# Relative-position attention on one core: eight PSUM banks shared out as 3 + 2 + 1 + 2 instead of 2 + 2 + 1 + 3

## The chip, the cores and the metric

The kernel runs on one core of a Trainium2 chip. The metric is the device time in microseconds. Lower is better. TensorE (PE in the profile) multiplies, VectorE (DVE), ScalarE (ACT) and GpSimd (POOL) do the rest, and SyncE (SP) issues the transfers. TensorE writes only to PSUM, which this program holds as eight banks of 128 x 512 fp32.

## The reference: what is computed

A layer on x of shape (8, 1024, 256), fp32, with 16 heads of width 16. The attention has relative-position terms for keys and for values, with distances clipped at 64 in both directions:

```python
q, k, v = proj(Wq, bq), proj(Wk, bk), proj(Wv, bv)        # of layernorm(x)
rk, rv = embK[idx], embV[idx]                              # idx = clip(j - i, -64, 64) + 64
logits = einsum('bhqd,bhkd->bhqk', q, k) + einsum('bhqd,qkd->bhqk', q, rk)
w = softmax(logits)
out = einsum('bhqk,bhkd->bhqd', w, v) + einsum('bhqk,qkd->bhqd', w, rv)
x = x + layernorm(out @ Wo.T + bo)
x = x + layernorm(x @ ternary(W).T + bias)                 # its input is layernorm(x) too
```

## The kernel before

**Steps.** The work is cut into 128 steps: 8 batches, 2 groups of 8 heads, 8 tiles of 128 queries (shifted by 64). Each step handles one tile of queries of 8 heads against all 1024 keys. Four steps form a group of four (`quad`), about 80 us long, 32 in all.

**What a step does.** First, several steps ahead, a row maximum is found. `row_max` (L919 on TensorE) multiplies a cut-down q and k, two heads side by side in the array, into two scores banks: four pairs of heads times two halves of the keys make 8 units, so 16 banks' worth. VectorE reduces each bank to a maximum: halves with the relative band by one fused instruction on scores plus `bands` (L1222, followed by a read of its accumulator), the other halves by a plain maximum (L1216). `row_maxed` counts the emptied banks. `max_rows` (L929) turns the negated maxima, and they are written into the q operand. Then `weights` (L946, with L950 adding the band) computes transposed logits in 16 blocks of 128 x 512, per half of the heads ("blk" 0 and 1) four of kind X and four of kind Y. The first two X blocks are "near": each of their four bf16 matmuls has an fp32 transpose of a band behind it. The others are "far", of four matmuls. ScalarE takes the exponential of each block (L1424) into `wl` and `wm` for near blocks, and `wr` and `wy` for far ones. `weighted` (L970) multiplies by the values into the bank `oacc`, X after the four X blocks, Y after the four Y blocks. `merge` (L1245) folds `wl` into `wm`.

**Small products.** Everything else TensorE does goes through the banks called `misc`, one user at a time: `band_raw` (L902, read by ScalarE in two copies, L1403 and L1404), `max_rows` (L929, read at L1235 and L1237), at the end of a group of four `relative` (L982, two parts of four pieces each, read by L1254 into `relout`) and `relative_sum` (L995, read by L1263), `out_norm` (L1006, read up to L1279), per finished tile of rows the tail products (L1020 read by L1437, L1034 read by L1292 or L1333), and per chunk of 256 tokens of the next batch the projections (L865, L875, L883, L892).

**Banks.** `NLOG, NMISC, NSCORE` give the counts for logits, small products and scores; `oacc` is the eighth bank. In `row_max` TensorE waits, for side 0 and 1 of the unit that starts with bank number u:

```python
pe.wait_ge(row_maxed, u + side - NSCORE + 1)
mm = e.matmul(scores[(u + side) % NSCORE][:, c % 512:c % 512 + length], ...
```

**What sets the order.** Each engine runs one fixed list of instructions, in order. `timetable` gives every stage of every step a place on a common scale (one unit is one head of one step; 32 units for a group of four) from the table `PLACES`; `order_of` sorts each engine's list by place plus the engine's lag from `LAG` (`END_LAG` for the last four tiles). `with_banks` goes through the stages in that order, gives each small product the bank that is free first, takes it as occupied for `HOLD` units, and pushes a product to a later place where no bank is free by this plan. `misc_banks` then finds for each the count of the reader that it must wait for. `HOLD` is a planning number only: the waits in the program are on the real readers. SyncE's queue is one such list too, for every load, store and band transfer.

Of the kernel before, what the change touches and what calls it, by code (L numbers as in the profile page):

```python
# [11 lines left out]
ACT = mybir.ActivationFunctionType  # L12
# [33 lines left out]
LOWEST = -3.0e38  # L46
QRING, BRING, VRING, MRING = 5, 7, 3, 3
HB = HG // 2
NLOG, NMISC, NSCORE = 2, 3, 2


def tile_of(s):
# [51 lines left out]
def own_root(stage, k):  # L104
# [1 line left out]
    return k == (0, 0) if stage == "statistics" else last_tile(*k) and k[1] % 2 == 1  # L106


PLACES = {'chunk': (61.05, 71.03, 81.0, 91.0),
 'load_x': -8.23,  # L110
 'statistics': -5.34,
 'normalise': -2.6,
 'turn_x': 0.38,
 'project_q': 1.18,
 'project_v': 10.3,
 'far': 4.0,
 'write_q': 6.3,
 'project_k': 5.53,
 'write_far': 7.8,
# [1 line left out]
 'first_chunk': (-100.0, -90.0, -80.0, -70.0),  # L121
 'first_statistics': (-108.7, -102.4, -102.27, -102.4),
 'first_normalise': (-103.3, -99.5, -89.5, -79.5),
 'first_stages': (-0.27, 0.5, 2.6, 4.4, 4.8, 5.83, 6.2, 6.3),
 'keys_first_stages': (0.0, 4.0, 4.8, 0.0, 3.0, 8.5, 7.3, 5.33),
 'first_load_k': (-84.0, -73.9, -63.8, -62.01),
 'first_load_q': (-89.0, -77.2, -65.4, -53.6),
 'first_raw': -54.47,
 'step': 7.2,
 'half': 3.55,  # L130
 'load_k': (-41.8, -33.8, -25.8, -17.8),
 'first_load_mk': (-83.9, -73.8, -63.8, -63.5),
 'load_mk': (-41.7, -33.7, -25.7, -17.7),
 'load_mq': -21.5,
 'first_load_mq': (-88.17, -77.1, -65.3, -53.5),
 'load_q': -32.7,
 'raw': (-28.8, -25.4),
 'band_write': (-26.3, -22.8),
 'band_read': (-22.18, -20.26),
 'row_max': (-12.49, -11.62, -10.75, -9.88, -9.01, -8.14, -7.1, -6.4),  # L140
 'max_reduce': -6.0,
 'max_rows': -4.88,
 'max_move': -5.05,
 'near': (0.0, 0.4, 0.72, 0.98),
 'rest': (1.76, 2.1, 2.5, 2.9),
 'value_x': 2.3,
 'value_y': 4.1,
 'merge': 3.2,
 'out_copy': 7.6,
 'relative': (29.57, 31.07),  # L150
 'piece_by': 0.35,
 'sum': (33.0, 33.95),
 'norm': (35.6, 36.59),
 'tail': 38.0,
 'tail_by': 8.0,
 'tail_late_by': 6.5,
 'tail_load': -1.0,
 'tail_attT': 0.21,
 'tail_wo': 1.0,
 'tail_x1': 3.0,  # L160
 'tail_norm': 3.5,
 'tail_normed': 5.4,
 'tail_x1T': 10.15,
 'tail_ff': 11.3,
 'tail_out': 13.5,
 'tail_store': 15.82,
 'end': 36.6,
 'end_by': 0.65,
 'end_stages': (0.3, 0.41, 2.27, 2.4, 3.4, 4.3, 4.7, 7.0, 6.8)}


def timetable():

    slots, x_ = [], PLACES

# [92 lines left out]
def with_banks(slots):  # L268
# [12 lines left out]
    while queue:  # L281
        slot, i, planned, stage, k = queue.pop()
        chain, bank = chain_of(stage, k), None
        if slot < planned + late.get(chain, 0):
            put_back((planned + late[chain], i, planned, stage, k))
            continue
        if stage in HOLD:
            if stage == "relative" and k[2]:
# [8 lines left out]
            if stage == "relative":  # L297
                held = bank
            until[bank] = slot + (10 if stage == "relative" and k[2] < 3 else HOLD[stage])
        timed.append((slot, stage, k, bank))  # L300
# [5 lines left out]
 'DVE': {'project_v': 0.17,  # L306
         'out_norm': 0.7,
         'tail_wo': 0.7,
         'tail_x1': 1.06,
         'tail_norm': 1.4,  # L310
         'tail_normed': 3.2,
         'tail_out': 1.9},
 'ACT': {'turn_x': -0.23, 'far': 0.4, 'project_q': 1.2, 'band_raw': -0.04},
 'POOL': {'project_q': 3.4,
          'project_k': 2.0,
          'far': 2.0,
# [6 lines left out]

END_LAG = {'PE': {},
 'SP': {},
 'DVE': {'tail_wo': 0.28, 'tail_ff': 0.5},
 'ACT': {'tail_attT': 0.2, 'tail_x1T': 1.0},
 'POOL': {'tail_wo': 0.95, 'tail_norm': 0.35, 'tail_ff': 0.86}}

# [1 line left out]
def order_of(engine, slots):  # L331


    def lag(stage, k):
# [22 lines left out]
            "project_v": "v_ready", "band_raw": "praw_ready", "max_rows": "nm_ready", "relative": "rel_ready",  # L357
            "relative_sum": "o_added", "out_norm": "attn_ready", "tail_attT": "rows_ready", "tail_x1T": "rows_ready",
            "tail_wo": "lin_ready", "tail_ff": "lin_ready", "ternary": "threshold_ready"}
HOLD = {'turn_x': 0.8,  # L360
 'project_q': 2.0,
 'project_k': 2.0,
 'far': 1.4,
 'project_v': 1.8,
 'band_raw': 0.8,
 'max_rows': 0.9,
 'relative': 1.0,
 'relative_sum': 1.4,
 'out_norm': 1.83,
 'tail_attT': 0.6,  # L370
 'tail_x1T': 0.5,
 'tail_wo': 1.3,
 'tail_ff': 1.3,
 'ternary': 2.0}


def counts(orders):
# [1186 lines left out]
```

## Time and profile before

| | us |
|---|---|
| median of 3 runs | 2714.83 |
| lowest, highest | 2706.01, 2718.36 |
| the profiled execution, whole | 2715.1 |
| its span, first to last instruction | 2713.3 |
| TensorE matmul row busy | 2488.4 (92%) |
| TensorE weight loads busy | 1778.2 (66%) |
| VectorE busy | 2098.3 (77%) |
| ScalarE busy | 1563.9 (58%) |
| GpSimd busy | 949.4 (35%) |

The first 100 us or so fill the pipeline, with projections of the first batch and many transfers; the last 60 us finish the last rows. Between them the pattern of a group of four repeats. A matmul stands in the trace twice, as a weight load (PEld) and as a matmul (PE), whose end is modelled; in brackets stands the idle time of the row in front of it and who ended it.

### The profile page before, as it was taken

The numbers are of one execution on the slowest core, as the hardware profiler recorded it, in microseconds if no ns is written. First come the engines' busy times: TensorE is split into PE (matmuls) and PEld (weight loads), VectorE is DVE, ScalarE is ACT, GpSimd is POOL, SyncE is SP. The second block draws the span as 40 slices with busy tenths as digits, with TensorE's granted clock in tenths as the row PEclk, the third lists the DMA queues.
The fourth block names the chain that finished last, engine by engine and source line by source line (L and its number), as shares of the span: only waits on it lengthen the run. The fifth ranks groups of instructions, "written<-read, shape, count | busy, mean of one in ns | idle before, by whom it ended". The sixth has DMA issues, their size and how long they took to land. (4 is left out here: it accounts for less than half of the span.)

```text
span 2713.3 us, 101117 instructions
## 1 busy us (share of the span) xinstructions
PE 2488.4 (92%) x41858; PEld 1778.2 (66%) x41858; DVE 2098.3 (77%) x5306; ACT 1563.9 (58%) x2993; POOL 949.4 (35%) x2211
## 2 busy tenths in 40 slices
PE   5599999999999999999999999999999999999995
PEld 3266766667666676667666676666766667666664
DVE  5577778877888778877788777887778877787776
ACT  2266665566666555666556665556665655566652
POOL 3001533335342443424334253343524244341014
PEclk8699999999999999999999999999999999999997
DMA  6765674657656575566655666456764657656510
GB/s 162 210 162 160 184 185 132 163 161 204 167 148 168 156 196 155 148 164 178 183 140 157 172 187 177 138 145 167 209 168 132 164 168 192 164 141 178 142 42 29
DMA packets 696147, 434.22 MB, mean 160 GB/s; under 512 B 215847, under 2 KB 695431, under 8 KB 695559
## 3 DMA queue, kind: packets, MB, share of 16 engines
q1 hardware_dynamic: 695686, 427.75, 57.3%
q8 instruction: 330, 5.41, 0.9%
q14 instruction: 131, 1.07, 0.1%
HBM read 231.91 MB, written 194.92 MB: 157 GB/s over the span
## 5 line engine op out<-in xcount | busy, mean ns | idle before, releaser
L946 PE MATMUL logitsT<-qs,ks 98*128 98x128 bf16 (+1 forms) x8192 | 952.9, 222 | 31.5 <-ACT wr L1424 11.6
L1222 DVE CUSTOM_DVE_ANT_1 junk<-scores,bands 128x512 bf16<-128x512 f32 x988 | 680.3, 689 | 270.4 <-PE scores L919 115.4
L1424 ACT ACTIVATE wy<-logitsT 128x512 f32<-128x512 f32 x1024 | 589.5, 597 | 419.8 <-PE logitsT L946 408.7
L1216 DVE TENSOR_REDUCE maxes<-scores 128x1 f32<-128x512 f32 x1024 | 657.3, 683 | 173.3 <-PE scores L919 171.0
L946 PEld LDWEIGHTS logitsT<-qs,ks 98*128 98x128 bf16 (+1 forms) x8192 | 576.0, 99 | 306.6 <-issue 172.2
L919 PE MATMUL scores<-mks,mqs 48*128 48x256 bf16 (+6 forms) x3712 | 518.8, 291 | 121.1 <-DVE maxes L1216 62.5
L950 PE MATMUL logitsT<-ident,bands 128*128 128x128 f32 x2048 | 407.9, 280 | 0.0
L1424 ACT ACTIVATE wr<-logitsT 128x512 f32<-128x512 f32 x512 | 293.5, 596 | 163.6 <-PE logitsT L946 157.4
L919 PEld LDWEIGHTS scores<-mks,mqs 48*128 48x128 bf16 (+1 forms) x3712 | 162.9, 94 | 333.7 <-DVE maxes L1216 111.2
L1453 POOL TENSOR_SCALAR rs<-rs 128x1 int32<-128x1 int32 (+1 forms) x217 | 42.2, 195 | 898.9 <-DVE rs L1097 888.4
L950 PEld LDWEIGHTS logitsT<-ident,bands 128*128 128x128 f32 x2048 | 295.8, 144 | 24.9
L1458 POOL TENSOR_SCALAR rs<-rs 128x1 f32<-128x1 f32 x744 | 282.4, 382 | 64.9
L970 PE MATMUL oacc<-wy,vs 128*17 128x128 f32 (+1 forms) x9216 | 277.1, 264 | 0.7 <-ACT wy L1424 0.7
L1463 POOL TENSOR_SCALAR rs<-rs 128x1 f32<-128x1 f32 x744 | 217.5, 295 | 66.1
L970 PEld LDWEIGHTS oacc<-wy,vs 128*17 128x17 f32 x9216 | 207.1, 98 | 37.5 <-issue 9.4
L1424 ACT ACTIVATE wl<-logitsT 128x512 f32<-128x512 f32 x256 | 158.4, 619 | 117.7 <-PE logitsT L950 116.4
L1424 ACT ACTIVATE wm<-logitsT 128x512 f32<-128x512 f32 x256 | 154.3, 603 | 83.0 <-PE logitsT L950 78.4
L1403 ACT ACTIVATE praw<-misc 128x512 f32<-128x512 f32 x256 | 153.4, 599 | 64.7 <-DMA bs<-praw 44.0
L1245 DVE COPY_PREDICATED wm<-later,wl 128x512 f32<-128x512 int32 x224 | 175.7, 784 | 2.2 <-PE oacc L970 2.2
L970 PE MATMUL oacc<-wr,vs 128*17 128x128 f32 (+1 forms) x4608 | 161.6, 264 | 0.0
L1404 ACT ACTIVATE praw<-misc 128x512 f32<-128x512 f32 x256 | 156.3, 611 | 0.0
L970 PEld LDWEIGHTS oacc<-wr,vs 128*17 128x17 f32 x4608 | 118.1, 100 | 0.1
(147 smaller groups left out, 2977.5 us busy)
## 6 DMA issues: line engine op xcount, KB each, us to landing
bs<-praw SPq DMA_DIRECT2D x256, 512.0 KB, 4.3
bands<-bs SPq DMA_DIRECT2D x224, 512.0 KB, 4.4
ks<-kd SPq DMA_DIRECT2D x64, 384.0 KB, 4.8
qs<-qd SPq DMA_DIRECT2D x112, 192.0 KB
bands<-bs SPq DMA_DIRECT2D x128, 128.0 KB, 3.3
mks<-kd SPq DMA_DIRECT2D x128, 96.0 KB, 3.9
qd<-qparts SPq DMA_DIRECT2D x60, 192.0 KB, 2.6
kd<-kparts SPq DMA_DIRECT2D x60, 192.0 KB, 2.6
```

Of the source, the lines that this page charges most:

```text
L919: mm = e.matmul(scores[(u + side) % NSCORE][:, c % 512:c % 512 + length], mqs[i][HALF * side:HALF * side + depth, p, :], kk[HALF * side:HA ...
L946: mm = e.matmul(lt[:, j * P:(j + 1) * P], kk[0:depth, SLOT[HB * blk + j], kt * P:(kt + 1) * P], qs[i][0:depth, SLOT[HB * blk + j], :], sta ...
L950: mm = e.matmul(lt[:, j * P:(j + 1) * P], band[v % BRING][:, j, c * P:(c + 1) * P], ident[:], start=False, stop=True, is_transpose=True, s ...
L970: mm = e.matmul(oacc[32 * j:32 * j + VW, o0 + q0:o0 + q1], vs[m_ % VRING][:, int(right), kt, h, :], src, start=first and c == 0, stop=True ...
L1216: e.tensor_reduce(top, sc[:], AX.X, ALU.max).then_inc(row_maxed, 1)
L1222: e.tensor_tensor_reduce(junk[:], sc[:].rearrange("p (a c) -> p a c", a=2), banded, 1.0, LOWEST, ALU.add, ALU.max, top).then_inc(row_maxed, 1)
L1245: e.copy_predicated(right, mask.bitcast(I32), left).then_inc(merged, 1)
L1403: e.activation(dst[:, :, 0:P], src, ACT.Copy)
L1404: e.activation(dst[:, :, P:WIN], src[:, :, P - 1:P].broadcast_to([P, HB, P]), ACT.Copy).then_inc(praw_ready, 1)
L1424: e.activation(dst, src, ACT.Exp).then_inc(exp_ready, 1)
L1458: op = e.tensor_scalar(rs[k][:, 3, x:x + 1], rs[k][:, 2, x:x + 1], rs[k][:, 0, x:x + 1], rs[k][:, 2, x:x + 1], ALU.mult, ALU.mult)
L1463: op = e.tensor_scalar(rs[k][:, 2, x:x + 1], rs[k][:, 3, x:x + 1], 1.5, rs[k][:, 2, x:x + 1], ALU.add, ALU.mult)
```

## The change

The counts become `NLOG, NMISC, NSCORE = 2, 2, 3`: three scores banks used in turn, and two small banks. No instruction's arithmetic changes and no instruction is added or removed. With NSCORE 3 a unit's side 0 waits until all banks up to three before its own are emptied, where it was two.

The numbers of `PLACES`, `LAG`, `END_LAG` and `HOLD` are set anew. Most move by a few hundredths to tenths of a unit. Those that change orders visibly:

```diff
-NLOG, NMISC, NSCORE = 2, 3, 2
+NLOG, NMISC, NSCORE = 2, 2, 3
@@ PLACES
- 'near': (0.0, 0.4, 0.72, 0.98),
- 'rest': (1.76, 2.1, 2.5, 2.9),
+ 'near': (0.0, 0.76, 0.72, 0.98),
+ 'rest': (1.76, 2.1, 2.5, 2.77),
- 'first_load_mq': (-88.17, -77.1, -65.3, -53.5),
+ 'first_load_mq': (-83.18, -73.73, -61.06, -50.13),
- 'sum': (33.0, 33.95),
+ 'sum': (33.44, 34.25),
@@ HOLD
- 'band_raw': 0.8,
- 'max_rows': 0.9,
- 'relative': 1.0,
- 'relative_sum': 1.4,
+ 'band_raw': 0.2,
+ 'max_rows': 0.23,
+ 'relative': 0.25,
+ 'relative_sum': -0.12,
```

All entries of `HOLD` shrink in this way, so the plan lets a product follow its bank's last user sooner.

TensorE at the end of a group of four, where the two parts of `relative` (`misc<-wm,reltab`) stand between scores, a row turn (`misc<-ident,attn`) and the output projection (`misc<-wo,rowsT`). The number behind a name is the bank or buffer. Before:

```order
L1020 MATMUL misc1<-ident,attn0 128x128
L1020 MATMUL misc1<-ident,attn1 128x128
L982 MATMUL misc0<-wm,reltab 32x64 x16
L1034 MATMUL misc2<-wo,rowsT 128x256 x2
L919 MATMUL scores0<-mks0,mqs2 128x512
L919 MATMUL scores1<-mks0,mqs2 128x512
L982 MATMUL misc1<-wm,reltab 32x64 x24
```

And after:

```order
L982 MATMUL misc0<-wm,reltab 32x64 x16
L1034 MATMUL misc1<-wo,rowsT 128x256 x2
L919 MATMUL scores0<-mks0,mqs2 128x512
L919 MATMUL scores1<-mks0,mqs2 128x512
L982 MATMUL misc0<-wm,reltab 32x64 x24
```

The 16 end part 0 and the 24 are the first three pieces of part 1. Part 1 had bank 1, while part 0 was still being read in bank 0; now both use bank 0 one after the other. The row turn has moved up ahead of these rows.

TensorE a little later, inside a step, from the end of the second near block to the last X block. Before:

```order
L946 MATMUL logitsT1<-qs2,ks0 128x128
L950 MATMUL logitsT1<-ident,bands 128x128
L946 MATMUL logitsT0<-qs2,ks0 128x128 x4
L919 MATMUL scores0<-mks0,mqs2 128x512
L919 MATMUL scores1<-mks0,mqs2 128x512
L946 MATMUL logitsT1<-qs2,ks0 128x128 x4
```

After, with the first far block in front of the near one (whose four pairs are left out here but for the first):

```order
L1020 MATMUL misc1<-ident,zbuf0 128x128 x2
L982 MATMUL misc0<-wm,reltab 32x64 x8
L946 MATMUL logitsT1<-qs2,ks0 128x128 x4
L946 MATMUL logitsT0<-qs2,ks0 128x128
L950 MATMUL logitsT0<-ident,bands 128x128
```

The far block has moved ahead of the near block; behind the near block follow the scores unit and the last far block, as before.

VectorE at the same end of a group, at the reader of part 0 (`relout<-misc0`) between two reductions. Before:

```order
L1222 ISA maxes1 128x1
L1326 TENSOR_SCALAR zbuf0<-x1_0,mv2,rs2 128x256
L1254 TENSOR_TENSOR relout<-misc0,relmask 128x8x32x2
L1216 TENSOR_REDUCE maxes1<-scores0 128x1
L1216 TENSOR_REDUCE maxes1<-scores1 128x1
L1292 TENSOR_TENSOR ybuf<-misc2,bo 128x256
```

After:

```order
L1222 ISA maxes1 128x1
L1254 TENSOR_TENSOR relout<-misc0,relmask 128x8x32x2
L1326 TENSOR_SCALAR zbuf0<-x1_0,mv2,rs2 128x256
L1216 TENSOR_REDUCE maxes1<-scores0 128x1
L1216 TENSOR_REDUCE maxes1<-scores1 128x1
L1292 TENSOR_TENSOR ybuf<-misc1,bo 128x256
```

The reader has moved up by one operation.

## Rows read from the trace of the kernel before

**Rows 1.** The page, part 1: busy us, share of the span, instructions.

```profile
PE 2488.4 (92%) x41858; PEld 1778.2 (66%) x41858; DVE 2098.3 (77%) x5306; ACT 1563.9 (58%) x2993; POOL 949.4 (35%) x2211
```

**Rows 2.** Waits of the matmul row: us in total, times, longest us.

```profile
PE scores L919 <- DVE maxes L1216: 62.5, 200, 1.6
PE scores L919 <- DVE maxes L1222: 28.4, 65, 2.9
```

**Rows 3.** Waits of the weight loads, whole span.

```profile
PEld scores L919 <- DVE maxes L1216: 111.2, 274, 1.8
PEld logitsT L946 <- ACT wr L1424: 72.9, 237, 0.7
PEld scores L919 <- DVE maxes L1222: 72.2, 169, 3.2
...
PEld logitsT L946 <- ACT wy L1424: 20.3, 80, 0.6
...
PEld logitsT L946 <- ACT wm L1424: 13.3, 49, 0.9
```

**Rows 4.** Timeline: start us, us, engine, line, count, [idle before].

```profile
1101.23 0.70 PE L919 MATMUL scores<-mks,mqs 48*128 48x256 bf16 x4
...
1101.54 0.11 PEld L919 LDWEIGHTS scores<-mks,mqs 48*128 48x128 bf16 x3 [0.22 <-DVE maxes L1216]
```

**Rows 5.** Waits of the weight loads in the first 150 us.

```profile
PEld scores L919 <- DVE maxes L1222: 13.1, 13, 3.2
PEld scores L919 <- DVE maxes L1216: 9.4, 16, 1.8
```

**Rows 6.** Groups by line: out<-in, count | busy, mean ns | idle before.

```profile
L1222 DVE CUSTOM_DVE_ANT_1 junk<-scores,bands 128x512 bf16<-128x512 f32 x988 | 680.3, 689 | 270.4 <-PE scores L919 115.4 <-issue 58.3 <-DMA bands<-bs 26.2
L1216 DVE TENSOR_REDUCE maxes<-scores 128x1 f32<-128x512 f32 x1024 | 657.3, 683 | 173.3 <-PE scores L919 171.0
...
L1222 DVE DVE_READ_ACCUMULATOR2_ANT maxes<- 128x1 f32 x1024 | 84.6, 83 | 0.0
```

**Rows 7.** Waits of the weight loads in one group of four, 1071.4 to 1149.9.

```profile
PEld scores L919 <- DVE maxes L1216: 3.7, 9, 0.7
PEld scores L919 <- DVE maxes L1222: 2.4, 8, 0.6
```

**Rows 8.** Timeline of the weight loads of scores at that group's end.

```profile
1142.17 0.09 PEld L919 LDWEIGHTS scores<-mks,mqs 48*128 48x128 bf16 x1 [0.67 <-DVE maxes L1216]
1142.77 0.22 PEld L919 LDWEIGHTS scores<-mks,mqs 48*128 48x128 bf16 x5 [0.51 <-DVE maxes L1216]
1144.09 0.09 PEld L919 LDWEIGHTS scores<-mks,mqs 48*128 48x128 bf16 x1 [0.21 <-DVE maxes L1222]
1144.83 0.09 PEld L919 LDWEIGHTS scores<-mks,mqs 48*128 48x128 bf16 x1 [0.65 <-DVE maxes L1222]
```

**Rows 9.** Busy time by stretch: from:to, length, engines, clock, DMA share, GB/s.

```profile
1071.40:1149.90 78.50, 74.97 (x1240) 53.49 (x1238) 68.32 (x181) 47.27 (x90) 33.05 (x92) 1.00 0.49 137
1141.00:1149.00 8.00, 6.83 (x140) 4.41 (x141) 7.51 (x19) 3.06 (x6) 4.27 (x12) 1.00 0.23 76
```

**Rows 10.** Timeline: the reader of part 0 on VectorE, part 1 on TensorE.

```profile
1148.20 0.68 DVE L1254 TENSOR_TENSOR relout<-misc,relmask 128x512 f32<-128x512 f32 x1
1148.83 1.08 PE L982 MATMUL misc<-wm,reltab 128*32 128x64 f32 x48
```

**Rows 11.** Timeline: two exponentials in a row, and the logits behind them.

```profile
1113.16 1.25 ACT L1424 ACTIVATE wr<-logitsT 128x512 f32<-128x512 f32 x2 [0.66 <-PE logitsT L946]
1114.47 0.23 PEld L946 LDWEIGHTS logitsT<-qs,ks 101*128 101x128 bf16 x4 [0.41 <-ACT wr L1424]
```

**Rows 12.** Groups by line: the second of the two readers of `band_raw`.

```profile
L1404 ACT ACTIVATE praw<-misc 128x512 f32<-128x512 f32 x256 | 156.3, 611 | 0.0
```

**Rows 13.** Timeline of TensorE at the start.

```profile
82.67 0.61 PE L919 MATMUL scores<-mks,mqs 51*128 51x512 bf16 x2 [17.11 <-DMA mks<-kd]
```

More of the change, by code:

```diff
@@ L106, in own_root @@
     return k == (0, 0) if stage == "statistics" else last_tile(*k) and k[1] % 2 == 1
-PLACES = {'chunk': (61.05, 71.03, 81.0, 91.0),
+PLACES = {'chunk': (61.72, 71.69, 81.66, 91.62),
  'load_x': -8.23,
@@ L112 @@
  'normalise': -2.6,
- 'turn_x': 0.38,
+ 'turn_x': 0.25,
  'project_q': 1.18,
- 'project_v': 10.3,
- 'far': 4.0,
+ 'project_v': 10.09,
+ 'far': 4.52,
  'write_q': 6.3,
@@ L123 @@
  'first_normalise': (-103.3, -99.5, -89.5, -79.5),
[L124 to L127, printed above, removed]
+ 'first_stages': (-0.3, 0.47, 2.57, 4.15, 4.77, 5.8, 6.17, 6.83),
+ 'keys_first_stages': (0.0, 4.0, 4.8, 0.08, 3.0, 8.5, 7.3, 5.33),
+ 'first_load_k': (-83.61, -73.9, -63.8, -62.01),
+ 'first_load_q': (-89.0, -77.2, -64.9, -53.6),
  'first_raw': -54.47,
@@ L130 @@
  'half': 3.55,
- 'load_k': (-41.8, -33.8, -25.8, -17.8),
- 'first_load_mk': (-83.9, -73.8, -63.8, -63.5),
- 'load_mk': (-41.7, -33.7, -25.7, -17.7),
+ 'load_k': (-41.8, -33.8, -25.8, -17.84),
+ 'first_load_mk': (-83.13, -73.03, -63.03, -62.73),
+ 'load_mk': (-41.8, -33.7, -25.7, -17.91),
  'load_mq': -21.5,
- 'first_load_mq': (-88.17, -77.1, -65.3, -53.5),
+ 'first_load_mq': (-83.18, -73.73, -61.06, -50.13),
  'load_q': -32.7,
  'raw': (-28.8, -25.4),
- 'band_write': (-26.3, -22.8),
+ 'band_write': (-26.51, -22.8),
  'band_read': (-22.18, -20.26),
@@ L143 @@
  'max_move': -5.05,
- 'near': (0.0, 0.4, 0.72, 0.98),
- 'rest': (1.76, 2.1, 2.5, 2.9),
+ 'near': (0.0, 0.76, 0.72, 0.98),
+ 'rest': (1.76, 2.1, 2.5, 2.77),
  'value_x': 2.3,
- 'value_y': 4.1,
+ 'value_y': 4.12,
  'merge': 3.2,
- 'out_copy': 7.6,
+ 'out_copy': 7.74,
  'relative': (29.57, 31.07),
- 'piece_by': 0.35,
- 'sum': (33.0, 33.95),
- 'norm': (35.6, 36.59),
+ 'piece_by': 0.37,
+ 'sum': (33.44, 34.25),
+ 'norm': (35.47, 36.59),
  'tail': 38.0,
@@ L157 @@
  'tail_load': -1.0,
- 'tail_attT': 0.21,
+ 'tail_attT': -0.28,
  'tail_wo': 1.0,
@@ L161 @@
  'tail_norm': 3.5,
- 'tail_normed': 5.4,
+ 'tail_normed': 5.5,
  'tail_x1T': 10.15,
@@ L167 @@
  'end': 36.6,
- 'end_by': 0.65,
- 'end_stages': (0.3, 0.41, 2.27, 2.4, 3.4, 4.3, 4.7, 7.0, 6.8)}
+ 'end_by': 0.66,
+ 'end_stages': (0.3, 0.41, 2.11, 2.32, 3.4, 4.16, 4.7, 7.0, 6.85)}
 def timetable():
@@ L308 @@
          'tail_wo': 0.7,
-         'tail_x1': 1.06,
+         'tail_x1': 0.88,
          'tail_norm': 1.4,
@@ L312 @@
          'tail_out': 1.9},
- 'ACT': {'turn_x': -0.23, 'far': 0.4, 'project_q': 1.2, 'band_raw': -0.04},
+ 'ACT': {'turn_x': -0.23, 'far': 0.4, 'project_q': 1.2, 'band_raw': -0.13},
  'POOL': {'project_q': 3.4,
@@ L325 @@
  'SP': {},
- 'DVE': {'tail_wo': 0.28, 'tail_ff': 0.5},
+ 'DVE': {'tail_wo': 0.28, 'tail_ff': 0.5, 'tail_norm': 0.22, 'tail_x1': -0.12},
  'ACT': {'tail_attT': 0.2, 'tail_x1T': 1.0},
@@ L359 @@
             "tail_wo": "lin_ready", "tail_ff": "lin_ready", "ternary": "threshold_ready"}
[L360 to L364, printed above, removed]
- 'band_raw': 0.8,
- 'max_rows': 0.9,
- 'relative': 1.0,
- 'relative_sum': 1.4,
[L369 to L374, printed above, removed]
+HOLD = {'turn_x': 0.06,
+ 'project_q': 1.25,
+ 'project_k': 0.92,
+ 'far': 0.45,
+ 'project_v': 0.45,
+ 'band_raw': 0.2,
+ 'max_rows': 0.23,
+ 'relative': 0.25,
+ 'relative_sum': -0.12,
+ 'out_norm': 0.75,
+ 'tail_attT': 0.15,
+ 'tail_x1T': 0.12,
+ 'tail_wo': 0.75,
+ 'tail_ff': -0.34,
+ 'ternary': 0.5}
 def counts(orders):
```

## The prediction

> **What bounds the kernel now.** I read the page first [rows 1]: TensorE's matmul row is busy for 2488.4 of 2713.3 us, VectorE's for 2098.3. TensorE's own queue sets the time; VectorE is the next. Then I asked who TensorE waits for. Its matmul row waits for `maxes` (VectorE's row maximum, which frees a scores bank) for 62.5 + 28.4 = 90.9 us [rows 2]. That understates it, because matmul ends are modelled. The weight loads in front of the same matmuls wait 111.2 + 72.2 = 183.4 us for `maxes` in 274 + 169 waits, and those of `logitsT` wait 72.9 + 20.3 + 13.3 = 106.5 us for the exponentials [rows 3]. An instance: before 1101.54 the load waits 0.22 us for `maxes` while the matmul row reads as busy, 0.70 us for four matmuls [rows 4]. I take the load row as the real stall. Of the 183.4 us, 13.1 + 9.4 = 22.5 us lie in the first 150 us [rows 5], where other things set the pace; 161 us lie in the steady part. The rows of the small products name inputs that they wait for, hardly ever the reader of an earlier product, so three small banks are enough now.
>
> **Part 1, a third scores bank.** A unit of `row_max` fills two banks (two heads), and VectorE empties each in 0.683 us, or in 0.689 + 0.083 = 0.77 us with the bands [rows 6]. With two banks TensorE can be one unit ahead only when both are emptied; with three it gets one bank, so 0.68 to 0.77 us, more lead. How much of a wait this removes depends on whether waits stand alone or in trains, for within a train the lead is spent once. I counted in one group of four steps, 1071.4 to 1149.9: 17 waits, 3.7 + 2.4 = 6.1 us [rows 7]. Three places are larger than one bank: the train 0.67 + 0.51 + 0.21 + 0.65 = 2.04 us at 1142 to 1145 [rows 8], and two units with two waits each of the same kind, 0.80 us at 1105 and 0.74 at 1123. Taking 0.68 off each leaves 0.12 + 0.06 + 1.36 = 1.5 us; the others stand apart, are at most 0.50 us and go. So 4.6 of 6.1, three quarters, is removed: 0.75 x 161 = **-121 us**. From below it is three quarters of the matmul row's waits, 0.75 x 90.9 = -68, less a tenth for the head, -61; from above all 161.
>
> **Part 2, carry-over.** VectorE is busy 68.32 of 78.50 us in that group, and 7.51 of the 8.00 us from 1141 to 1149, across the train [rows 9]. Once TensorE comes earlier, VectorE's backlog is larger at the next unit, and part of the removed wait returns. Nothing shows how much: nothing at least, 50 us at most (then VectorE's idle time shrinks from 10.2 us a group by only 2.2). I take a fifth of part 1, **+25 us**.
>
> **Part 3, near and far blocks.** `near` moves the second near block (four pairs of bf16 and fp32 matmuls) from in front of the first far block to behind it, so the two far X blocks no longer stand together. Today they do: two exponentials take 1.25 us in a row, and the next block of logits waits 0.41 us for the bank at 1114.47 [rows 11]. In the new order the far block's exponential, 0.60 us, runs beside the near block. It also puts the second values product (`wy`) of the step before one near block sooner behind its exponentials; no wait of that kind stands in the rows now, and some may come. I take **-15 us** of the 106.5; bounds are -50 (about half of it) and +30, since TensorE, held up less by VectorE, reaches these two banks earlier and ScalarE's 0.6 us per block is unchanged.
>
> **Part 4, two small banks instead of three.** 990 small products pass through them. A bank comes free when the reader is done: for `band_raw` two copies of 0.6 us on ScalarE, for `relative` one of 0.68 us [rows 10, 12], with VectorE's queue in front: 1 to 2 us in all. I counted in the order, spacing TensorE's rows as the trace does, how much other work stands between a bank's use and its next use. Under 1.0 us: 11 products before, 28 after. Under 1.5 us: 19 and 118. Under 2.0 us: 50 and 219. The median falls from 6.0 to 3.6 us. The new places thus use the work between well but leave a hundred products at the limit. The case to look at is `relative`: part 1 now goes into the bank of part 0, and must wait for its reader. In the trace part 1 starts at 1148.83 and that reader ends at 1148.20 + 0.68 = 1148.88 [rows 10], so this costs little, and the reader moves ahead of one VectorE operation. About 118 x 0.3 us = **+35 us**. Bounds: 28 x 0.5 = +14; 219 x 0.5 = +110, if readers are late as behind VectorE's backlog at 1142.
>
> **Part 5, the rest.** `HOLD`, the lags and most places only decide the orders counted above. At the start, SP issues the q writes of a chunk ahead of loads of `mqs`, and `mks` behind the k writes. TensorE waits there until 82.67, 17.11 us, for `mks` [rows 13]; that comes from the last chunks, and the issues ahead of these are the same in number. 0, within 5 us either way. The last 60 us pass through two small banks instead of three; the tail of the last rows waits for normalisations, not for banks. 0, within 5 us.
>
> **Sum.** 2713.3 - 121 + 25 - 15 + 35 = 2637 us of span. The execution took 2715.1, so 1.8 us lie outside: 2639, rounded to **2640 us**. It is as good against the median, 2714.8, from which the profiled run differs by 0.3 us. A measurement of this kernel can tell about 0.5%, 13.6 us, from no change.
>
> **Rivals.**
> A, the full gain (10%). All waits for `maxes` go, part 3 gives its -30, and small banks cost their least: 2715 - 161 - 30 + 14 + 10 = 2548 us. For it: most waits are shorter than one bank's 0.68 us. Against it: the train at 1142. The Trainium skill (Perfetto Trace Analysis, Matmuls) says that independent matmul groups should rotate through different banks so that emptying one overlaps the next group; by that rule alone this would be the case to expect.
> B, VectorE is the bound (13%). The gain is the lower end of part 1, -61, then +25 for the carry-over and +35 for the banks: 2715 - 61 + 60 = 2714 us, no change. For it: 87% of VectorE busy in the group shown. Against it: elsewhere it is less, and 10.2 us of idle time are left in this group.
> C, slower (12%): the small banks stop TensorE's queue. A small product that waits holds up all logits and scores behind it, VectorE and ScalarE run dry, the backlog then delays the next reader. At 219 products x 0.8 us = 175 us, less 121, with 25 carried over, it gives 2715 + 79 = 2794 us. It decides from 96 us of new waits on, 0.44 us for each of the 219. Against it: the places leave a median of 3.6 us. The Trainium skill (Perfetto Trace Analysis, Optimization Strategy) reads the same gap, repeated on the engine that should be full, as a sign of too few PSUM buffers; the trace shows it today at the scores and not at the small products, and the rule warns of both.
>
> **How the numbers follow.** The forecast, 65%, has 2590 to 2690 as its own range. A is 10%, B 13%, C 12%. The range 2575 to 2712 holds the forecast's case with its tails, half of B and a part of A; C and the far end of A are left out. Faster by over 0.5% (under 2701): 0.65 + 0.10 + 0.01 = 0.76. Within 0.5%: 0.12. Slower: 0.12.
>
> **What would show it.** In the profile after: loads of `scores` waiting for `maxes` about 50 to 80 us instead of 183.4 (part 1 with its carry-over), what is left standing at the end of each group of four steps; `logitsT` loads waiting 70 to 110 us for ScalarE; new rows of small products waiting for `praw`, `nm`, `relout`, `vs` or `attn`, together about 35 us and none over 15. VectorE's busy share should rise from 77% to 79 or 80. I am wrong in part 1 if the `maxes` waits stay above 110 us, and in part 4 if small products wait over 70 us.

## The result, and the profile after

The kernel after takes **2569.24 us** (median of 4, 2568.3 to 2575.28), the kernel before 2710.73 in the same comparison (median of 4, 2706.01 to 2718.36). The ratio is **0.948**, with 0.945 to 0.951 as its 95% interval: 141.5 us less. The forecast was 2640, its low end 2575. So the sign was right, and the time is 6 us below the range. One of the ten executions behind experiment x1 below ran at a mean clock of 0.646 and took 3245.83 us; it is left out of every number here.

The page after, part 1 (rows 1 are the same line of before):

```profile
PE 2413.4 (94%) x41858; PEld 1747.5 (68%) x41858; DVE 2072.1 (81%) x5306; ACT 1564.0 (61%) x2993; POOL 955.9 (37%) x2211
```

The instruction counts are the same. The span is 2568.1 us, 145.2 less. TensorE's busy time fell by only 75.0 us (its row can read as busy while a load waits, as [rows 4] showed), and its idle time by 70.2. VectorE's share is 81%, where I had forecast 79 or 80.

The waits of the weight loads after (us in total, times, longest us), to be held against [rows 3]:

```profile
PEld logitsT L946 <- ACT wr L1424: 59.0, 243, 0.4
...
PEld scores L919 <- DVE maxes L1222: 30.2, 67, 1.3
PEld scores L919 <- DVE maxes L1216: 29.2, 80, 1.0
...
PEld logitsT L946 <- ACT wm L1424: 23.7, 103, 0.4
...
PEld misc L982 <- DVE relout L1254: 9.9, 14, 1.0
...
PEld misc L995 <- DVE relout L1254: 6.6, 10, 3.4
```

The waits for `maxes` fell from 111.2 + 72.2 = 183.4 us to 29.2 + 30.2 = 59.4. This -124 is the largest change of any wait. Of it, 13 lie in the first 150 us (22.5 to 9.5, [rows 5]) and 111 behind them (160.9 to 49.9). `logitsT` waits for ScalarE went from 106.7 us (the 106.5 of [rows 3] and 0.2 for `wl`) to 59.0 + 23.7 + 11.3 (`wy`) + 1.7 (`wl`) = 95.7. Against both stands a wait that before did not have: `relative` (L982) waits for `relout`, 9.9 us in 14 waits. The matmul row understates here as it did in [rows 2]; after, it shows

```profile
PE scores L919 <- DVE maxes L1216: 12.6, 39, 0.8
PE scores L919 <- DVE maxes L1222: 10.8, 22, 1.0
```

**Where along the span.** The first group of four starts at 113 us in both kernels, and the end takes 110 and 109 us. All of the gain is therefore in the groups of four. They come in four kinds, by what else they carry; the shortest of each kind took 78.4, 75.9, 85.3 and 79.5 us before and 74.9, 70.5, 83.2 and 76.0 after. Two neighbours in the windows view (from:to, length, busy time and count of PE, PEld, DVE, ACT, POOL, clock, DMA share, GB/s):

```profile
1022.60:1097.50 74.90, 73.13 (x1239) 52.47 (x1236) 67.47 (x181) 47.55 (x90) 33.10 (x92) 1.00 0.54 153
1097.50:1168.30 70.80, 68.33 (x1340) 49.39 (x1332) 58.98 (x151) 46.09 (x85) 17.45 (x46) 1.00 0.69 190
```

Before, the first of them is the first of [rows 9], and the second this:

```profile
1149.90:1228.20 78.30, 73.67 (x1335) 52.10 (x1334) 59.45 (x151) 46.92 (x87) 18.42 (x47) 0.96 0.62 170
```

In the first group VectorE's busy time is nearly the same (68.32 and 67.47 us) and the group is 3.6 us shorter, so VectorE now fills 90% of it (67.47 of 74.90), where it was 87%. In the second the gain is 7.5 us; note the clock, 0.96 before and 1.00 after.

The train of [rows 8] at the end of the first group has become this (timeline of the weight loads):

```profile
1090.26 0.22 PEld L919 LDWEIGHTS scores<-mks,mqs 48*128 48x128 bf16 x5 [0.60 <-DVE maxes L1216]
...
1092.09 0.09 PEld L919 LDWEIGHTS scores<-mks,mqs 48*128 48x128 bf16 x1 [0.42 <-DVE maxes L1222]
...
1096.51 0.89 PEld L982 LDWEIGHTS misc<-wm,reltab 128*32 128x32 f32 x48 [0.69 <-DVE relout L1254]
```

2.04 us of waits for `maxes` are now 0.60 + 0.42 = 1.02, so 1.02 went, more than one bank's 0.68. The sum over the group is 1.8 + 0.8 = 2.6 instead of 6.1 [rows 7]; beside the train six single waits of 0.19 to 0.49 us are left. The last row is a price of having only two small banks: part 1 stands still for 0.69 us until part 0 is read out.

### The profile page after: what moved, and what is told of

It is laid out like the page before. It is cut to its first block, busy times and chain, and to the rows that moved or that the text cites. A ratio compares the mean times of both kernels' runs of the same rounds, so it can differ in the third digit from the quotient of the medians.

```text
span 2568.1 us, 101028 instructions
## 1 busy us (share of the span) xinstructions
PE 2413.4 (94%) x41858; PEld 1747.5 (68%) x41858; DVE 2072.1 (81%) x5306; ACT 1564.0 (61%) x2993; POOL 955.9 (37%) x2211
## 4 chain that ended last, share of the span: by engine, by line
PE 54%; DVE 13%; issue 4%; ACT 3%; POOL 1%; DMA 0%; SPq 0%; DVEq 0%; ACTq 0%; POOLq 0%
PE logitsT L946 13%; PE oacc L970 12%; PE scores L919 7%; PE logitsT L950 6%; DVE junk L1222 4%; DVE maxes L1216 4%; PE misc L1034 3%; PE misc L875 3%; PE misc L995 2%; PE misc L892 2%; PE misc L902 1%; ACT wr L1424 1%; PE misc L982 1%; DVE stats L1092 1%; PE misc L1006 1%
## 5 line engine op out<-in xcount | busy, mean ns | idle before, releaser
L946 PE MATMUL logitsT<-qs,ks 98*128 98x128 bf16 (+1 forms) x8192 | 915.7, 221 | 21.8 <-ACT wr L1424 8.8
L1424 ACT ACTIVATE wy<-logitsT 128x512 f32<-128x512 f32 x1024 | 581.4, 597 | 332.3 <-PE logitsT L946 321.1
L946 PEld LDWEIGHTS logitsT<-qs,ks 98*128 98x128 bf16 (+1 forms) x8192 | 562.4, 99 | 274.9 <-issue 150.4
L919 PE MATMUL scores<-mks,mqs 48*128 48x256 bf16 (+6 forms) x3712 | 448.5, 289 | 36.8 <-DVE maxes L1216 12.6
L1424 ACT ACTIVATE wr<-logitsT 128x512 f32<-128x512 f32 x512 | 305.3, 596 | 200.2 <-PE logitsT L946 191.6
L1453 POOL TENSOR_SCALAR rs<-rs 128x1 int32<-128x1 int32 (+1 forms) x217 | 48.6, 224 | 803.3 <-DVE rs L1097 793.8
L919 PEld LDWEIGHTS scores<-mks,mqs 48*128 48x128 bf16 (+1 forms) x3712 | 138.9, 94 | 196.9 <-DVE maxes L1222 30.2
L1424 ACT ACTIVATE wm<-logitsT 128x512 f32<-128x512 f32 x256 | 152.9, 597 | 24.6 <-PE logitsT L950 3.8
L902 PE MATMUL misc<-bandtab,qs 96*128 96x128 bf16 x1024 | 100.3, 220 | 20.3 <-ACT praw L1404 14.5
```

Of the source, the lines that this page charges most:

```text
L946: mm = e.matmul(lt[:, j * P:(j + 1) * P], kk[0:depth, SLOT[HB * blk + j], kt * P:(kt + 1) * P], qs[i][0:depth, SLOT[HB * blk + j], :], sta ...
L1424: e.activation(dst, src, ACT.Exp).then_inc(exp_ready, 1)
```

## The experiments

The runs are called x1 to x12. **The theory** (L in the expectations) was the prediction's with a larger first term: the third scores bank is worth well over 100 us, the two small banks cost little, and the new orders alone bring little. **Its rival** (O): the orders brought the gain, and the banks only came along. Two facts of the program make a clean table possible. The new tables give the same order of instructions on every engine whether the counts are 2, 2, 3 or 2, 3, 2 or 2, 2, 2 (only the numbers of the banks differ), and the old tables with the new `HOLD` keep TensorE's order of before but for a few products at the very end. So order and banks can be changed apart.

### New order, two scores banks and two small ones

```diff
 # after
-NLOG, NMISC, NSCORE = 2, 2, 3
+NLOG, NMISC, NSCORE = 2, 2, 2
```

> The changed kernel with NLOG, NMISC, NSCORE = 2, 2, 2: the new orders, two small banks, and the third scores bank taken away again. The instruction order of each engine is the changed kernel's, only the waits differ. Theory L (the lead of the third bank carries the gain, about 105 to 125 us of it, the clock's dips with it): 2680 to 2700 us, weight loads of scores waiting 150 to 190 us for maxes. Theory O (the new orders carry most of the gain, the bank little): 2590 to 2620 us, with waits for maxes under 100 us.

Measured (x1): 2698.79 us (median of nine), ratio to before 0.9959 (0.994 to 0.9979).

```profile
PEld scores L919 <- DVE maxes L1216: 109.1, 274, 1.2
PEld scores L919 <- DVE maxes L1222: 92.3, 224, 1.3
```

201.4 us of waits for `maxes` against 59.4 after: 142 us, and the time differs by 130 us. The waits are above the 150 to 190 us that I expected. In the matmul row the same waits are 62.0 + 36.8 = 98.8 us, against 23.4 after: 75 us, which is too little for the 130.

### New order, banks shared out as before

```diff
 # after
-NLOG, NMISC, NSCORE = 2, 2, 3
+NLOG, NMISC, NSCORE = 2, 3, 2
```

> The changed kernel with the counts of before, 2, 3, 2: the new orders alone. Theory L: 2665 to 2690 us, so 20 to 45 us under the kernel before, from fewer costly neighbours on TensorE and the near and far blocks; it lies 0 to 20 us under the run with 2, 2, 2, which is the price of the small bank. Theory O: 2580 to 2610 us.

Measured (x2): 2691.91 us, ratio 0.9927 (0.9903 to 0.995), just above the range. The orders alone give 20 us. The third small bank is worth 7 us in this order, which is not told apart from none: the intervals of x1 and x2 overlap. The waits for `maxes` are 109.6 + 95.9 = 205.5 us, 22 more than before: what the new order saves elsewhere, TensorE partly gives back at the scores banks.

### Old order, banks shared out as after

```diff
 # before
-NLOG, NMISC, NSCORE = 2, 3, 2
+NLOG, NMISC, NSCORE = 2, 2, 3
 # and HOLD as after
```

> The kernel before with the counts 2, 2, 3 and the new HOLD, which leaves TensorE's order as it was but for the last few products: the banks alone. Theory L: 2590 to 2630 us; the waits for maxes fall from 183 to 60 to 90 us, small products wait 10 to 40 us more. Theory O: 2680 to 2710 us. If the third bank and the new orders only work together, it stays above 2660 although the run of new orders alone does too.

Measured (x3): 2629.03 us, ratio 0.9693 (0.9664 to 0.9722).

```profile
PEld scores L919 <- DVE maxes L1216: 42.3, 96, 1.6
PEld scores L919 <- DVE maxes L1222: 26.7, 79, 1.1
PEld misc L982 <- DVE relout L1254: 24.5, 27, 1.4
```

### Old order, two banks for all

```diff
 # before
-NLOG, NMISC, NSCORE = 2, 3, 2
+NLOG, NMISC, NSCORE = 2, 2, 2
 # and HOLD as after
```

> The kernel before with 2, 2, 2 and the new HOLD: the order of before with one small bank less and nothing for it. The prediction put this price at 35 us (14 to 110): 2725 to 2820 us. If small banks are as cheap as the profile after suggests, 2715 to 2730 us. Beside the run with the old order and 2, 2, 3 it gives the worth of the third scores bank a second time.

Measured (x4): 2738.08 us, ratio 1.0104 (1.0073 to 1.0135). `relative` waits 12.0 us for `relout` here, and small products in all 88 us instead of 47.5. The matmul row's waits for `maxes` are 87.3 us here and 24.6 in x3: again too little, 63 us, for the 109 us between the two runs.

**The table these four complete** (medians in us; in brackets the weight loads' waits for `maxes`):

| logits, small, scores | old order | new order |
|---|---|---|
| 2, 3, 2 | 2712 (183) | 2692 (206) |
| 2, 2, 2 | 2738 (179) | 2699 (201) |
| 2, 2, 3 | 2629 (69) | 2569 (59) |

Down the last step, the third scores bank is worth 109 us in the old order and 130 in the new one, and the waits for `maxes` fall by 110 and 142: nearly one for one. Some of it is clock: the mean granted clock in the middle of the runs is 0.973 in x4 and 0.977 to 0.978 in x3, 0.976 in x1 and 0.979 after, by my estimate 12 and 8 us. The step above it, the third small bank given up, costs 26 and 7 us. Across, the new order brings 20 us with 2, 3, 2, then 39 with 2, 2, 2 and 60 with 2, 2, 3. So the theory stands for the banks: -20 + 7 - 130 = -143. Its part on the orders was too small. They are worth 21 us more with the third scores bank than without it, and 19 us more with two small banks than with three.

### What in the orders: the near and far blocks

```diff
 # after
- 'near': (0.0, 0.76, 0.72, 0.98),
+ 'near': (0.0, 0.4, 0.72, 0.98),
```

> The changed kernel with near set back to (0.0, 0.4, 0.72, 0.98): both near blocks in front of both far X blocks again, the rest as changed. The prediction gave this edit 15 us: 2575 to 2595 us. If the 60 us between the old order and the new order with three scores banks (2629 and 2569) lie mostly in near, 2610 to 2630 us.

Measured (x5): 2579.05 us, ratio 0.9501 (0.9483 to 0.952): 10 us more than after by the medians, 6 by the ratios, whose intervals overlap. `logitsT` waits for ScalarE 98.4 us against 95.7.

```diff
 # before, with the banks and HOLD of after
- 'near': (0.0, 0.4, 0.72, 0.98),
+ 'near': (0.0, 0.76, 0.72, 0.98),
```

> The kernel before with 2, 2, 3, the new HOLD and only near set anew: near alone on the old order. If near is most of the 60 us, 2570 to 2590 us. If it is the 15 us of the prediction, 2605 to 2625 us, and the rest lies in the places of scores and small products.

Measured (x6): 2624.22 us, ratio 0.9657 (0.9628 to 0.9687), against 0.9693 without the edit. The two runs point the same way and each alone is within its uncertainty. A small gain, some 5 to 10 us.

### What in the orders: three groups of places, each put into the kernel of x3

First the projections of the next batch (`chunk` moves their loads, statistics and stores with them):

```diff
 # before, with the banks and HOLD of after
-PLACES = {'chunk': (61.05, 71.03, 81.0, 91.0),
+PLACES = {'chunk': (61.72, 71.69, 81.66, 91.62),
- 'turn_x': 0.38,
+ 'turn_x': 0.25,
- 'project_v': 10.3,
- 'far': 4.0,
+ 'project_v': 10.09,
+ 'far': 4.52,
```

> The old order with 2, 2, 3 (2629 us) and only the places of the projections set anew (chunk, turn_x, project_v, far). Between that kernel and the changed one lie 60 us; the near blocks gave 5 to 10 of them. If the rest lies in the places of small products, this run takes a part: 2605 to 2625 us, with the waits of small products at 80 to 95 us instead of 102.

Measured (x9): 2594.97 us, ratio 0.9559 (0.9531 to 0.9587), 34 us less than 2629.03 and 10 us below the range that I expected.

```profile
PEld misc L982 <- DVE relout L1254: 10.4, 14, 1.1
```

`relative`'s waits for `relout` go from 24.5 us in 27 waits to 10.4 in 14, all waits of small products from 102 to 79 us. Nothing of `relative` itself was moved, only the work of the projections, some of which uses the same two banks. The waits that are gone stood at two of a batch's four groups of four, 9.4 us in the one with most of the projections and 5.4 in the one at whose end they begin; the other two have 9.6 us in x3 and 10.5 in x9. So more than half of that stall hung on where the projections stand. Whether they took `relative`'s bank or delayed its reader in VectorE's queue, this run does not separate.

Then the small products of the step and the tail (`piece_by`, `sum`, `norm`, `out_copy`, `tail_attT`, `tail_normed`, the `end` places, `LAG`, `END_LAG`):

```diff
 # before, with the banks and HOLD of after
- 'sum': (33.0, 33.95),
- 'norm': (35.6, 36.59),
+ 'sum': (33.44, 34.25),
+ 'norm': (35.47, 36.59),
...
- 'tail_attT': 0.21,
+ 'tail_attT': -0.28,
```

> The old order with 2, 2, 3 and the places of the other small products set anew: relative, its sums, out_norm, the tail, and the lags. Expected if the order around relative and its reader is the cost of two small banks: 2590 to 2615 us, loads of relative waiting for relout 8 to 15 us instead of 24.5. If it stays above 2620, the 60 us lie elsewhere.

Measured (x10): 2633.65 us, ratio 0.9708 (0.9683 to 0.9734). No gain: 5 us more than x3, not told apart from none. The waits for `maxes` fell by 15 us (53.9 against 69.0) and the time did not follow. The trace shows two things behind that. It has 30.7 us at half clock in its steady part, where x3 has 10.2. And the four kinds of groups went different ways (the shortest full one of each, taken here from the last load of `relative` to the next): the kind without projections and the one at whose end they begin are shorter than in x3, 75.2 against 75.8 us and 70.7 against 71.3; the kind with most of them and the one in which they end are longer, 87.3 against 86.2 and 77.7 against 76.9.

And the logits' and values' places:

```diff
 # before, with the banks and HOLD of after
- 'near': (0.0, 0.4, 0.72, 0.98),
- 'rest': (1.76, 2.1, 2.5, 2.9),
+ 'near': (0.0, 0.76, 0.72, 0.98),
+ 'rest': (1.76, 2.1, 2.5, 2.77),
- 'value_y': 4.1,
+ 'value_y': 4.12,
```

> The old order with 2, 2, 3 and near, rest and value_y set anew, the whole order of logits. near alone gave 5 us (2624). rest moves one far Y block by 0.13 units, so that two Y blocks stand together before the scores unit: 2605 to 2625 us. If it falls under 2600, the order of logits against scores is the larger part of the 60 us.

Measured (x11): 2622.90 us, ratio 0.9667 (0.9641 to 0.9693), as with `near` alone. Of the 60 us between x3 and after, the projections carry 34, these places some 6, the small ones none by themselves. About 20 us belong to no group alone. By the same measure after is shorter than x9 in all four kinds of groups, by 0.4 to 0.9 us each (70.8 to 70.1, 83.8 to 83.4, 76.9 to 76.1, 75.8 to 74.9); eight groups of each come to some 22 us. That fits small products whose gain of 0.6 us a group in x10 shows once the projections stand elsewhere. It was not tested, and the load places, which none of the three had, may have a part; this stays open.

### The waits for `maxes` themselves, shortened at their source

Both kernels with the plain maximum over a quarter of its bank, which makes VectorE's reader faster and leaves the banks as they are:

```diff
 # before (x7) and after (x8), L1216
-  e.tensor_reduce(top, sc[:], AX.X, ALU.max).then_inc(row_maxed, 1)
+  e.tensor_reduce(top, sc[:, 0:128], AX.X, ALU.max).then_inc(row_maxed, 1)
```

> The kernel before, but the plain maximum (L1216) reads 128 of the 512 columns of its bank, so the row maximum leaves out three quarters of half of the keys; TensorE's work is unchanged. VectorE gets some 450 us less work. Theory L (the weight loads' waits for maxes, 183 us, are what the two banks cost): waits fall under 60 us and the time to 2560 to 2600 us. If the matmul row's 91 us were the true size, it would stay at 2620 or above.

Measured (x7): 2581.23 us, ratio 0.951 (0.9492 to 0.9527).

```profile
PEld scores L919 <- DVE maxes L1222: 49.4, 108, 3.2
...
PEld scores L919 <- DVE maxes L1216: 6.4, 21, 0.8
```

The load row's waits for `maxes` fall by 183.4 - 55.8 = 127.6 us and the time falls by 134. The matmul row had only 90.9 us of such waits to give [rows 2]. The near match is not exact evidence: VectorE also has 393 us less work (2098.3 to 1705.5), and other waits of the load row rise (`logitsT` and `oacc` for ScalarE by 18 us, transfers by 28). But x4 against x3 and x1 against after, where only a bank changes, say the same, 110 and 142 us of waits for 109 and 130 us of time. So the load row has nearly the true size of this stall, and the matmul row half of it.

> The changed kernel with the same short maximum (L1216 reads 128 of 512 columns; three quarters of half of the keys are left out of the row maximum). Waits for maxes are 59 us there now. Theory L: they fall to 10 to 30 us and the time to 2525 to 2550 us, 20 to 45 us under the changed kernel. If VectorE still sets the pace of the changed kernel through other waits, it gains over 60 us.

Measured (x8): 2524.82 us, ratio 0.9295 (0.9269 to 0.9321): 44 us less than after, where 26 us of the waits for `maxes` go (59.4 to 33.4) and 14 of small products' waits (76.7 to 62.6). So a faster VectorE is still worth something after the change, a third of what it was, and by these waits the scores banks are some 26 us of the 44.

### A value product one step of the table sooner

```diff
 # after
- 'value_x': 2.3,
+ 'value_x': 2.0,
```

> The changed kernel with value_x at 2.0 instead of 2.3: the first values product between the first and the second Y block, where TensorE waits for ScalarE today (27 us before the second Y block). If that wait is hidden by it: 2545 to 2565 us. If the product itself now waits for the last X exponential, and the later Y blocks stand closer together: 2570 to 2600 us, with more waits of oacc for ScalarE.

Measured (x12): 2631.57 us, ratio 0.9695 (0.967 to 0.972), 62 us more than after. A miss in size.

```profile
PEld logitsT L946 <- ACT wy L1424: 73.0, 205, 0.6
...
PEld oacc L970 <- ACT wr L1424: 36.6, 132, 0.5
```

The value product now stands ahead of its exponential (`wr`) and waits 132 times; behind it in TensorE's queue stand logits, so ScalarE gets its next block late, and then the logits wait for `wy`, 73.0 us where after has 11.3. Moving one stage by 0.3 units costs almost half of what the third bank brings.

## Why the prediction was right or wrong

**The reading of the bound was right.** TensorE's queue set the time, and its largest stall was the wait for `maxes`, 183.4 us by the load row. The pairs x4 and x3, x1 and after confirm the choice of the load row.

**The sizes of the waits that I had priced came near.** What was missing lies outside them. Each is taken from the sums of the weight loads' waits, before and after:

| | forecast | measured |
|---|---|---|
| parts 1 and 2: `scores` for `maxes`, from 150 us on | -121 + 25 = -96 | 160.9 to 49.9: -111 |
| the same in the first 150 us | left out | 22.5 to 9.5: -13 |
| part 3: `logitsT` for ScalarE | -15 | 106.7 to 95.7: -11 |
| part 4: small products for readers and inputs on VectorE and ScalarE | +35 | 47.5 to 76.7: +29 |
| values (`oacc`) for ScalarE | named in part 3, not priced | 2.7 to 11.4: +9 |
| everything else | 0 | -48 |

The "else" completes the span's 145.2 us: the load row's own busy time is 30.7 us less (1778.2 to 1747.5, the same 41858 loads), waits for transfers are 7 less, waits named "issue" 4 less, and 7 lie in gaps too short to be listed.

**Part 5, everything else at 0, is the first step that failed.** By this table 48 us lie there. Two things had no term of their own.

One is the orders: "most places only decide the orders counted above". I had priced one visible swap, at -15, and added it to the banks as if neither depended on the other. The new order is worth 20 us with the banks of before, 39 with two banks for each use and 60 with the banks of after. 34 of these 60 are the projections', to whose places I gave no term. They stand mostly in one of the four kinds of groups, but in x3 more than half of `relative`'s 24.5 us of waits for its bank went when they alone were moved. A little of what they give is the clock: the trace of x3 has 10.2 us at half clock in its steady part, that of x9 none, so 5 us at most.

The other is the clock. The mean granted clock is 0.971 in the middle of 14 runs of before (0.965 to 0.976) and 0.979 in those of after; 0.008 of some 2640 us is about 20 us, an estimate. I looked for waits alone, and the sum had no term for it. It is not all of the busy time that the load row lost: the profiled executions of x1 and after have the same mean clock, 0.979, and the loads take 1768.0 and 1747.5 us. So some 20 of the 30.7 us came with the third scores bank at an equal clock; why the loads themselves get shorter with fewer waits is not shown.

**Part 2, the carry-over, is the second: a guess, too large.** In the group that I had priced it fits: 3.5 of 6.1 us went, and 4.6 less a fifth is 3.7. The train kept 1.02 us where 1.36 was expected, but six single waits stayed that were to go. Over the whole steady part 69% of the waits went (111 of 160.9), more than the 60% that three quarters less a fifth come to, and so 10 of the 25 us are left for a carry-over. The 13 us of the first 150 us were left out although the third bank works there too. The prediction also contradicted itself: it expected 50 to 80 us of these waits to be left, and 183.4 less the gross 121 is 62, with the charge 87. The Trainium skill (Perfetto Trace Analysis, Matmuls) says to rotate independent matmul groups through different PSUM banks. This case agrees, with 109 to 130 us for a third bank.

**Part 3 came near partly by luck.** `near`, the edit that it priced, gives 3 us of these waits in the new order (98.4 in x5, 95.7 after) and 5 in the old one (114.5 in x3, 109.2 in x6). The third scores bank in the old order adds 9 (105.6 in x4, 114.5 in x3), as the reason for the upper bound had it; the rest of the new order takes that back.

**Part 4, the two small banks, was right in kind, and its size is luck.** The waits are +29 us against +35, and the row named ahead, `relative` for its bank, is the largest of its kind, 9.9 us; no new one is over 15. But from x2 to x1, where only the third small bank goes, they rise by 14.5 us (45.9 to 60.4), and another 16.3 come with the third scores bank (60.4 to 76.7). As time in the table the bank costs 26 us in the old order and 7 in the new, where the clock may give some back (0.973 in the middle of x2's runs, 0.976 of x1's, 8 us by estimate). The count of products with under 1.5 us of other work between two uses of a bank, on which I put the price, is 108 in x3, 101 in x9 and 118 after, with waits of 102, 79 and 77 us, and says nothing of this. The count under 1.0 us (72, 58 and 28) falls with them, but it does not fix them either: x4 has the order and the small banks of x3 and waits for 88 us.

**The two sums side by side.** Forecast: -96 for the third bank with its carry-over, +35 for the small bank, -15 for the orders: -76. Measured by the table: -143, and how it is shared out depends on the path. With the new order first it is -20 + 7 - 130; then of the 67 us between the sums the third bank has 34, the small bank 28, the orders 5. With the banks first it is +26 - 109 - 60; then they have 13, 9 and 45. The 40 us that change sides are what the changes give only together (21 with the third scores bank, 19 with the small one), and a sum of independent terms has no place for them.

**The rivals.** A, the full gain, with 2548 us, is the nearest of the three in time, but its mechanism did not happen: 59.4 us of waits for `maxes` are left, and x8 shows that a faster reader still gives 44 us. Its sum also takes -30 from part 3, whose bounds are -50 and +30, and a +10 without a source. B falls: VectorE's share went up to 81% and the gain came. C falls at these places: with the old ones, x4, the waits of small products rise by 40 us and the time by 26, far from the 175 of C's sum. x12 shows what it takes to get to a loss of C's kind: a product that waits 132 times costs 62. The range was too narrow below because it let neither the clock nor the orders give anything beyond the terms that I had counted.

## What to carry to other kernels

Give a spare PSUM bank to the use whose reader the weight loads wait for longest, and price it by the load row: here 110 and 142 us of waits taken away gave 109 and 130 us of time. A change of banks and a new order have to be valued together: the same new order gave 20 us with the banks of before and 60 with those of after. A rare stage can cost much where it shares banks and engines with others, so give its place a term in the forecast too (here 34 us).

## What the runs showed of the hardware

The granted clock also falls in a kernel whose TensorE is busy for 92% of the time. In the steady part of before the trace has 54.4 us at the half level, 1.2 of 2.4 GHz, in 12 short stretches, four of them some 321 us apart, once per batch (near 244, 565, 886 and 1207 us). One of them, in the windows view:

```profile
561.50:565.10 3.60, 2.46 (x24) 1.28 (x22) 2.88 (x7) 2.17 (x4) 0.00 (x0) 1.00 0.92 283
565.10:568.50 3.40, 3.40 (x77) 2.84 (x76) 2.95 (x9) 0.60 (x2) 1.89 (x6) 0.50 0.58 163
568.50:572.00 3.50, 3.50 (x90) 2.55 (x88) 2.54 (x6) 2.55 (x5) 3.09 (x9) 1.00 0.00 0
```

What TensorE did ahead of the fall, in the timeline:

```profile
562.45 0.28 PE L919 MATMUL scores<-mks,mqs 48*128 48x256 bf16 x1 [0.23 <-DVE maxes L1216]
563.05 0.39 PE L919 MATMUL scores<-mks,mqs 48*128 48x256 bf16 x3 [0.32 <-DVE maxes L1216]
...
564.97 0.52 PE L919 MATMUL scores<-mks,mqs 51*128 51x512 bf16 x1 [0.45 <-DVE maxes L1222]
```

Few matmuls (24 in 3.6 us, where the next two windows have 77 and 90) with waits for `maxes` between them, in a stretch where transfers also run densely (DMA share 0.92). The trace of after has no such stretch in its steady part. The profiles of the others have 47.6 us (x2), 34.0 (x4), 3.4 (x1), 10.2 (x3), none (x9). These are single executions, and the clock differs between executions of one kernel: 0.972 to 0.979 in the nine of x1, of which the profiled one is the highest. So they do not tell what the banks and the order each do to the clock. That the waits cause the falls was not tested either; it is read from where they stand, and x1, with more waits for `maxes` than before (201.4 us) and 3.4 us at half clock, shows that their sum does not decide it.

The clock also goes with how runs of one kernel differ. Of 14 runs of before, the one with the lowest mean clock, 0.965, took 2726.86 us and one with the highest, 0.976, 2702.65: 24 us for 0.011, where 0.011 of the span is 30.
